# A six-layer decoder on one core: masks of 64 contraction rows in pairs, split first loads, reordered entries into the expert layers, and PSUM banks dealt out anew in the last attention

## The chip, the cores and the metric

The kernel runs on one core of one Trainium2 chip, as one program launched once. The metric is the device time of that launch in microseconds. Before the change it is 1089.61 us, the median of 3 runs (1089.28 to 1089.79).

The engines are named as in the profile: PE is TensorE's matmuls, PEld its weight loads, DVE is VectorE, ACT ScalarE, POOL GpSimd and SP SyncE, which here only issues DMAs.

## What is computed

The input x is 8 batches of 128 tokens with 256 features, the context has the same shape. Six layers follow each other, and after each stands `x = layernorm(x + layer(x))`:

```
A  self-attention, 16 heads of 16, causal
B  attention to the context, 16 heads of 16, plus a residual through relu(x W)
C  experts: 64 of 96 units, the 8 best per token, routed by softmax
D  linear attention in chunks of 64 tokens: running sums of k v and k, gate, rotary embedding
E  attention, 32 query heads of 8 over 8 key heads, keys are the context's and x's,
   scores + ALiBi, window of 64 tokens on the context and 32 on x, then softmax
F  experts: 8 of 176 units, the 2 best per token, plus a shared expert of 704 units with a sigmoid gate
```

The masks of A and E are added to the scores before the softmax: 0 where a key is seen, -1e30 where not. In E only keys up to 64 tokens back are seen. So the 64 early queries of a batch need the early keys only, and the late queries need all of them.

## The kernel before, in words

Every engine has one instruction stream, written out by hand and tied to the others by semaphores. `pe_self_cross` (layers A and B), `pe_moe("C")`, `pe_linear_cross` (D and E) and `pe_moe("F")` are TensorE's; the others have functions of the same kind. Items are batches, and the loops over `t` run stages of different batches side by side.

**Loads.** SyncE issues the constants' and weights' DMAs in groups, `load_weights` (L346): group A (x transposed, head mask, all weights of layer A, and two tiles `v` with their columns of ones), then A2 (causal mask, identities, x by rows), then B, then the first four expert blocks. TensorE, VectorE and ScalarE wait for the whole of group A at their start, TensorE waits for A2 before the first scores, GpSimd for A2 before the first residual.

**Layer A.** One item on TensorE is: keys, values and queries projected (fp32, `pe_T` L411 and `pe_rows` L418), for each of four PSUM banks the causal mask as a bf16 matmul with the identity as weights, 128 rows and 512 columns (L479), then the scores on top, with heads in four row groups of 32 (L485), transposes of the exponentials (L493), values (L524), and output steps (L534, L541). An fp32 matmul has two records in the trace.

**Into an expert layer.** `pe_moe` starts with the routing: the combine weights are transposed in two halves (`pe_combine_T`, L970), ScalarE copies them to `cT`, and `pe_token_weights` (L981) spreads them for the first two blocks. When both halves of `cT` are there, SyncE writes them to DRAM, reads them back spread (L310), and, in layer C, issues all loads of layers D and E (L320) before it refills the expert weights (L284). GpSimd splits every block of weights into a high and a low part (L1977, L1979). A block is 12 matmuls for gate and up (L995) per half of the tokens and 6 for down (L1012). Down accumulates in four banks, which are first cleared by four matmuls with a tile of zeros (L1030).

**Layer D.** `project` begins each of its two halves with a bias matmul of 33 contraction rows in fp32r (L626) and goes on with two fp32 matmuls of 128 rows (L628). `sums` (L647) and `numerators` (L661) use quarters and halves of the array by `tile_position`.

**Layer E.** For each batch there are 12 steps k. In iteration t, scores of one batch (`scores`, for the row maxima, which VectorE reduces, L1649 and L1653) and transposed scores of the batch before it (`scores_T`, of which ScalarE takes the exponentials, L1289) alternate. Steps with k % 3 = 0 are for early queries, the others for late ones. Each begins with a mask matmul of 128 rows and 512 columns (L788 or L796; L829 or L836) and adds the scores with 100 or 102 rows (L792 with four matmuls of 128 columns, L799 with two of 256; L832 and L840 with two of 256). Scores have a ring of two banks, transposed scores of three. Between the steps stand the queries of the next batch (L745, k = 2), its keys and values (L757, L764, k = 4), values (L861, k = 1 and 7), and output steps. SyncE moves each batch's queries and keys between partitions (`spread_queries` L364, 12 DMAs; `spread_keys` L375, 6 DMAs), and then puts the maxima as two rows under the queries (`maxima_rows`, L385); the transposed scores' first step waits for those. VectorE multiplies queries with the head masks (L1637); the scores' first step waits for that.

## Time and profile before

| what | value |
|---|---|
| median of 3 runs | 1089.61 us (1089.28 to 1089.79) |
| the profiled execution | 1087.74 us, its span 1085.9 us |
| mean granted clock of TensorE | 0.96 |
| busy: PE, PEld | 993.8 us (92%), 785.1 us (72%) |
| busy: DVE, ACT, POOL | 617.8 us (57%), 430.2 us (40%), 319.8 us (29%) |
| chain that ended last, by engine | PE 81%, SPq 5%, DVE 5%, issue 3%, DMA 2%, ACT 2%, POOL 1% |
| layers A and B, C, D, E, F, roughly | 0 to 185, 185 to 615, 615 to 710, 710 to 912, 912 to 1086 us |

The profile follows one execution; its times are microseconds from the start of the span. A row of the timeline gives start, duration, engine, line, operation, written and read tiles with their shapes, how many instructions are merged, and, in brackets, how long the engine was idle before and what released it. The chain of waits is followed backwards from the last instruction: each piece is what the end waited for at that time. The ends of matmuls are modelled, their starts are not, so lengths are best read from start to start. At the full granted clock (2.4 GHz) matmuls of 512 columns in fp32r or bf16 follow each other after 0.21 to 0.23 us here (12 of L995 take 2.72 us of the chain), that is about a column per clock, and each of the two records of an fp32 matmul takes about twice that (0.43 us in layer D).

### The profile page before, as it was taken

To read this page: it belongs to the slowest core of one execution; us is meant where nothing else is said; L and a number is where in the kernel's file an instruction comes from. 1 tells how busy PE (TensorE), PEld (TensorE's weight loads), DVE (VectorE), ACT (ScalarE), POOL (GpSimd) and SP (SyncE) were. 2 spreads that over 40 slices of the span, in tenths; PEclk is the share of its full clock that TensorE was granted. 3 is DMA by queue.
4 is the path that set the end of the run, shared out by engine and by line. 5 is a ranking of instruction groups with operands and counts; after the bars stand their busy time and mean duration, and the time that the engine had idled before them with its cause. 6 is when DMAs were issued, how large, how long until landed. Compare 5 with 4: busy or idle time off the path is not lost.

```text
span 1085.9 us, 18386 instructions
## 1 busy us (share of the span) xinstructions
PE 993.8 (92%) x6139; PEld 785.1 (72%) x6148; DVE 617.8 (57%) x1035; ACT 430.2 (40%) x839; POOL 319.8 (29%) x530
## 2 busy tenths in 40 slices
PE   4999997969999999999999689868999998999994
PEld 3778885658888888888888335557787776688883
DVE  2666777435555555555556457554555563455555
ACT  2777785413223223223222223224555554323221
POOL 0033124214443443443444301110000014234431
PEclk9999998989999999999999789978999999899998
DMA  8000000464333333333330000011111101264511
GB/s 298 2 2 2 2 2 2 94 177 140 129 115 117 110 111 119 107 110 120 109 106 15 9 1 1 17 27 27 25 25 31 32 11 59 59 183 106 120 31 39
DMA packets 36950, 75.74 MB, mean 70 GB/s; under 512 B 6844, under 2 KB 17960, under 8 KB 36498
## 3 DMA queue, kind: packets, MB, share of 16 engines
q1 hardware_dynamic: 36606, 74.77, 23.8%
q8 instruction: 34, 0.56, 0.2%
q0 software_dynamic: 288, 0.23, 0.2%
q14 instruction: 22, 0.18, 0.1%
HBM read 67.80 MB, written 2.40 MB: 65 GB/s over the span
## 4 chain that ended last, share of the span: by engine, by line
PE 81%; SPq 5%; DVE 5%; issue 3%; DMA 2%; ACT 2%; POOL 1%; DVEq 0%; POOLq 0%; ACTq 0%
PE ps L995 31%; PE ps L1012 15%; PE ps L411 4%; PE ps L628 3%; PE ps L418 3%; PE ps L493 3%; SPq L364 2%; SPq L320 2%; PE ps L861 2%; PE ps L485 2%; PE ps L524 2%; PE ps L745 1%; PE ps L836 1%; PE ps L840 1%; PE ps L796 1%
## 5 line engine op out<-in xcount | busy, mean ns | idle before, releaser
L995 PE MATMUL ps<-shared 128*128 128x512 f32 x1560 | 381.2, 394 | 9.5 <-POOL shared L1979 9.5
L995 PEld LDWEIGHTS ps<-shared 128*128 128x128 f32 x1560 | 296.9, 191 | 74.0 <-issue 11.7
L1397 ACT ACTIVATE shared<-pT 128x512 fp32r<-128x512 f32 x130 | 82.1, 632 | 287.4 <-DVE pT L1815 287.4
L1977 POOL CAST shared<-wraw 128x512 fp32r<-128x512 f32 (+1 forms) x130 | 92.0, 708 | 315.1 <-PE ps L1012 288.5
L1818 DVE TENSOR_TENSOR al<-pT,shared 128x512 fp32r<-128x512 f32 x130 | 117.1, 901 | 104.3 <-ACT shared L1397 104.3
L1012 PE MATMUL ps<-shared 128*128 128x512 f32 x520 | 162.4, 394 | 1.3 <-DVE al L1818 1.2
L1807 DVE TENSOR_TENSOR e<-e,ps 128x512 f32<-128x512 f32 x130 | 89.3, 687 | 128.4 <-PE ps L995 128.1
L1979 POOL TENSOR_TENSOR shared<-wraw,shared 128x512 fp32r<-128x512 f32 (+1 forms) x130 | 132.3, 1017 | 10.4
L1873 POOL TENSOR_SCALAR newton<-agg 128x1 f32<-128x1 f32 (+1 forms) x36 | 9.1, 254 | 384.1 <-DVE agg L1442 357.5
L1012 PEld LDWEIGHTS ps<-shared 128*128 128x128 f32 x520 | 98.4, 190 | 23.4 <-DVE al L1818 2.1
L1391 ACT ACTIVATE e<-ps 128x512 f32<-128x512 f32 x130 | 77.7, 597 | 84.3 <-PE ps L995 84.2
L1815 DVE TENSOR_TENSOR pT<-e,kbd 128x512 f32<-128x512 f32 x130 | 99.0, 761 | 10.0 <-DMA kbd<-combine_C 3.0
L1012 PE MATMUL ps<-al,shared 128*128 128x512 f32 x260 | 101.8, 392 | 0.0
L1012 PEld LDWEIGHTS ps<-al,shared 128*128 128x128 f32 x260 | 49.2, 189 | 10.3
L1458 DVE TENSOR_REDUCE mx<-ps 128x8 f32<-128x1024 f32 x32 | 39.0, 1220 | 22.2 <-PE ps L485 22.2
L1653 DVE TENSOR_REDUCE mcol<-ps 128x2 f32<-128x512 f32 x64 | 43.2, 677 | 6.0 <-PE ps L799 5.7
L411 PE MATMUL ps<-c_x_t,arena 128*128 128x128 f32 x192 | 28.2, 291 | 14.4 <-DMA v<-in_A_ones_v 12.4
L1137 ACT ACTIVATE pT<-ps 128x512 f32<-128x512 f32 x64 | 36.4, 598 | 8.0 <-PE ps L493 7.9
L799 PE MATMUL ps<-kT,shared 100*128 100x256 f32 x128 | 39.4, 391 | 0.0
L1466 DVE TENSOR_TENSOR e<-ps,mx 128x1024 f32<-128x1024 f32 x32 | 39.0, 1220 | 0.6
L411 PEld LDWEIGHTS ps<-c_x_t,arena 128*128 128x128 f32 x192 | 24.5, 197 | 20.3 <-DMA v<-in_A_ones_v 12.4
L1289 ACT ACTIVATE e<-ps 128x512 f32<-128x512 f32 x48 | 28.4, 595 | 26.6 <-PE ps L832 14.9
(225 smaller groups left out, 1447.5 us busy)
## 6 DMA issues: line engine op xcount, KB each, us to landing
kbd<-combine_C SPq DMA_DIRECT2D x46, 512.0 KB
wraw<-in_C_w SPq DMA_DIRECT2D x48, 384.0 KB, 8.1
kbd<-combine_F SPq DMA_DIRECT2D x15, 512.0 KB
wraw<-in_F_w SPq DMA_DIRECT2D x17, 384.0 KB, 7.1
kbd<-kbd SPq DMA_DIRECT2D x96, 32.0 KB, 1.9
kT<-kbd SPq DMA_DIRECT2D x48, 32.0 KB, 1.8
c_x_t<-in_x_t SPq DMA_DIRECT2D x1, 1024.0 KB, 4.9
c_x_rows<-in_x_rows SPq DMA_DIRECT2D x1, 1024.0 KB, 7.0
```

The lines of the kernel that those rows point to most:

```text
L411: mm = pe.matmul(dst[:, c * P:(c + 1) * P], w[:, k, c * P:(c + 1) * P], src[:, k, :], start=(k == 0), stop=(k == C - 1))
L799: mm = pe.matmul(bank[:, o * D:(o + 1) * D], q_[0:KR, g, 1, o * P:(o + 1) * P], k_[t][0:KR], start=False, stop=True, skip_group_check=True)
L995: mm = pe.matmul(GU[t][s], w[u][:, (c * 2 + s) * P:(c * 2 + s + 1) * P], xx[:, c, t * HALF:(t + 1) * HALF], start=(i == 0), stop=(i == 5))
L1012: mm = pe.matmul(Y[:, 2 * m + t, :], w[u][:, (4 + m) * P:(5 + m) * P], x_[t][:, :], start=False, stop=False, skip_group_check=True)
L1391: act.activation(sgt[t], GU[t][0], ACT.Silu).then_inc(S("silu"), 1)
L1397: act.activation(ah[t][:, :], a2[t], ACT.Copy).then_inc(S("ah"), 1)
L1653: dve.reduce_max(m4[:, g0 + k % 3 - 1, 1, :], SRING[n % 2].rearrange("p (o k) -> p o k", o=2), AX.X)\
L1807: dve.tensor_tensor(a1[t], sgt[t], GU[t][1], ALU.mult).then_inc(S("m_a1"), 1)
L1815: dve.tensor_tensor(a2[t], a1[t], wbc[k][:, t * HALF:(t + 1) * HALF], ALU.mult)\
L1818: dve.tensor_tensor(al[t][:, :], a2[t], ah[t][:, :].bitcast(F32), ALU.subtract)\
L1977: pool.tensor_copy(wh[u][:, lo:hi], wraw[k][:, lo:hi]).then_inc(S("m_wh"), 1)
L1979: pool.tensor_tensor(wl[u][:, lo:hi], wraw[k][:, lo:hi], wh[u][:, lo:hi].bitcast(F32), ALU.subtract).then_inc(S("m_wl"), 1)
```

## The change

It has five parts. (1) The causal mask is now one tile of 128 x 128 per parity of the bank (the second one has its halves of rows swapped); each bank gets it by two matmuls of 64 rows and 64 output partitions, which lie in quarters of the array. (2) In layer E all masks lie in one tile `windows`, by query in partitions 0 to 63, by key in 64 to 127. A score mask uses rows 0 to 63 and a transposed-score mask rows 64 to 127, both 128 output partitions wide, and they are issued one behind the other; steps with k % 3 other than 0 are cut in two halves of 256 columns, each with its own masks and scores. All waits of both kinds stand ahead of the masks. (3) Scores have three banks, transposed scores two. (4) The first loads are four groups A0 to A3, and the ones in `v` are written by GpSimd. Layer B's masked biases are made at t = 6 instead of t = 2. (5) At the entries into the expert layers, gate and up matmuls are cut in two and issued in another order, down begins its banks with `start` instead of the four clearing matmuls, and ScalarE's `high` comes earlier.

```diff
-            load_weights("A")
-            load_weights("A2")
+            for group in ("A0", "A1", "A2", "A3"):
+                load_weights(group)
...
+        XT = sb("c_x_t", [P, C, T])
+        loads["A0"] = [(XT[:, :, 0:2 * P], a["x_t"][:, :, 0:2 * P])]
+        hmask = const("A0", "head_mask")
+        causal = [const("A2", f"causal{h}_bf16", BF16) for h in range(2)]
...
+        loads["A2"].append((X[:, 0:2, :], a["x_rows"][:, 0:2, :]))
+        loads["A3"] = [(XT[:, :, 2 * P:], a["x_t"][:, :, 2 * P:]), (X[:, 2:, :], a["x_rows"][:, 2:, :])]
...
+        for group, names in (("A0", "wk bk"), ("A1", "wv bv wq bq"), ("A2", "bo wo")):
...
-        smask = [const("E", f"smask{h}_bf16", BF16) for h in range(2)]
-        tmask = [const("E", f"tmask{h}_bf16", BF16) for h in range(2)]
+        windows = const("E", "windows_bf16", BF16)
...
-        SRING = [ps[:, 1 + n, :] for n in range(2)]
-        TRING = [ps[:, 3 + n, :] for n in range(3)]
+        SRING = [ps[:, 1 + n, :] for n in range(3)]
+        TRING = [ps[:, 4 + n, :] for n in range(2)]
...
                     for r in range(4):
-                        pe.matmul(ps[:, r, :], ident16[:, :], causal[:, :], start=True, stop=False, skip_group_check=True)
+                        for n in range(2):
+                            rows, out = bass.ds(64 * n, 64), 64 * (n ^ r % 2)
+                            pe.matmul(ps[out:out + 64, r, :], ident16[rows, rows], bc(causal[r % 2][rows, :], 1, 4),
+                                      start=True, stop=False, tile_position=(64 * n, out), skip_group_check=True)
...
+                if t == 2 * B + 3:
+                    pe.wait_ge(S("pc"), 8 * B)
+                    pe_gate_up(pe, "C", 0, 0, 0, (0,))
                 if lo:
                     values(t - 3, 1)
...
-                    pe.wait_ge(S("pc"), 8 * B)
-                    pe_gate_up(pe, "C", 0, 0, 0)
...
+            def scores_mask(b, k, h):
...
+                if k % 3 == 0:
+                    pe.matmul(SRING[n % 3], windows[0:64, 0:P], bc(windows[0:64, P:2 * P], 1, 4),
+                              start=True, stop=False, tile_position=(0, 0), skip_group_check=True)
+                else:
+                    pe.matmul(SRING[n % 3][:, h * D:(h + 1) * D], windows[0:64, 0:P], windows[0:64, 2 * P:4 * P],
+                              start=True, stop=False, tile_position=(0, 0), skip_group_check=True)
...
+            def scores_T_mask(b, k, h):
...
+                    if n >= 2:
+                        pe.wait_ge(S("E_exp"), n - 1)
...
+                lo, n_q, at_ = (0, 8, 0) if k % 3 == 0 else (P + h * P, 4, h * D)
+                pe.matmul(TRING[n % 2][:, at_:at_ + n_q * 64], windows[64:128, lo:lo + P],
+                          bc(ident16[64:128, 64:128], 1, n_q), start=True, stop=False, tile_position=(64, 0),
+                          skip_group_check=True)
...
-                    if es is not None:
-                        scores(es, k)
-                    if ev is not None:
-                        scores_T(ev, k)
+                    for h in range(1 if k % 3 == 0 else 2):
+                        if es is not None:
+                            scores_mask(es, k, h)
+                        if ev is not None:
+                            scores_T_mask(ev, k, h)
+                        if es is not None:
+                            scores(es, k, h)
+                        if ev is not None:
+                            scores_T(ev, k, h)
...
-            gate_up(0, 0, 1)
-            gate_up(1, 1, 0)
+            if L == "C":
+                pe_gate_up(pe, L, 0, 0, 0, (1,))
+            pe_gate_up(pe, L, 0, 0, 1, (0,))
             pe_combine_T(pe, BEFORE[L], 1)
+            pe_gate_up(pe, L, 0, 0, 1, (1,))
             pe_token_weights(pe, L, 0, 1)
             pe_token_weights(pe, L, 1, 1)
-            before_done(pe, L)
-
-            pe.wait_ge(S("zero16"), 1)
-            pe.wait_ge(S("m_spread"), 4 * (L == "F") + 4)
-            for m in range(4):
-                pe.matmul(Y[:, m, :], ident16[:, :], zero16[:, :], start=True, stop=False, skip_group_check=True)
+            gate_up(1, 1, 0)
+            pe.wait_ge(S("m_spread"), 4 * (L == "F") + 2)
             down(0, 0, 0)
             gate_up(1, 1, 1)
+            before_done(pe, L)
+            pe.wait_ge(S("m_spread"), 4 * (L == "F") + 4)
             down(0, 0, 1)
...
             act_combine_T(act, BEFORE[L], 1)
+            high(0, 0)
             act_token_weights(act, L, 0, 1, 3)
+            gate(0, 1)
             act_token_weights(act, L, 1, 1, 4)
+            high(0, 1)
             before_done(act, L)
-            high(0, 0)
-            gate(0, 1)
-            high(0, 1)
...
-            loaded(pool, "A")
+            for u in range(2):
+                pool.memset(v[u][:, :], 0.0).then_inc(S("v_one"), 1)
+            pool.wait_ge(S("v_one"), 2)
+            for u in range(2):
+                pool.memset(v[u][:, :].rearrange("p (h w) -> p h w", w=VW)[:, :, DH0:DH0 + 1], 1.0).then_inc(S("v_one"), 1)
```

The other lines of the diff place the waits: values and queries of item 0 wait for A1 (ScalarE's and VectorE's parts of them too), keys of item 2 and the residual of item 2 for A3.

## Rows read from the trace of the kernel before

**Rows 1.** The chain of waits, first microseconds (start, duration, what).

```profile
6.31 6.07 DMA v<-in_A_ones_v
```

**Rows 2.** Timeline, TensorE and SyncE, entry into layer C.

```profile
200.52 0.60 PE L970 MATMUL ps<-c_ident,oT 128*64 128x128 f32 x4
...
227.44 0.90 SPq L320 DMA_DIRECT2D c_smask_bf<-in_smask_bf  x2
...
238.26 4.55 PE L995 MATMUL ps<-shared 128*128 128x512 f32 x12 [9.49 <-POOL shared L1979]
```

**Rows 3.** Busy time by engine, one steady batch of layer E (stretch, its length, PE busy, ...).

```profile
765.20:788.20 23.00, 21.63 (x196) 17.93 (x195) 13.56 (x27) 12.19 (x25) 2.62 (x6) 1.00 0.13 29
```

**Rows 4.** Timeline, SyncE's queue, steady batch of layer E.

```profile
767.55 8.43 SPq L364 DMA_DIRECT2D kbd<-kbd  x12
...
780.58 0.53 SPq L385 DMA_DIRECT2D shared<-mlo  x1
```

**Rows 5.** DMA issues of the whole run (times issued, KB each, us to landing).

```profile
shared<-mlo SPq DMA_DIRECT2D x16, 8.0 KB, 1.8
...
arena<-in_A_wk SPq DMA_DIRECT2D x1, 256.0 KB, 5.5
```

**Rows 6.** The chain of waits, steady batch of layer E.

```profile
773.51 0.40 PE ps L792 x4
...
774.38 0.23 PE ps L796
774.62 0.23 PE ps L799 x2
774.85 0.23 PE ps L836
775.09 0.24 PE ps L840 x2
...
783.34 0.38 PE ps L788
```

**Rows 7.** Timeline, TensorE's matmuls in layer D.

```profile
664.67 0.67 PE L661 MATMUL ps<-oT,qT 64*64 64x128 f32 x16
...
666.28 1.98 PE L628 MATMUL ps<-arena,c_x_t 128*128 128x512 f32 x4
668.20 0.50 PE L626 MATMUL ps<-shared 33*128 33x512 f32 x1
668.63 1.99 PE L628 MATMUL ps<-arena,c_x_t 128*128 128x512 f32 x4
```

**Rows 8.** Timeline, TensorE's weight loads in the same stretch.

```profile
667.25 0.19 PEld L628 LDWEIGHTS ps<-arena,c_x_t 128*128 128x128 f32 x1 [0.24 <-issue]
668.20 0.18 PEld L626 LDWEIGHTS ps<-shared 33*128 33x128 f32 x1 [0.76 <-issue]
```

**Rows 9.** Who waited for whom, TensorE, 765.2 to 788.2 us (total, times, longest).

```profile
PE ps L788 <- DVE shared L1637: 1.4, 1, 1.4
```

**Rows 10.** The chain of waits, end of layer E's second iteration.

```profile
757.66 1.78 DMA shared<-mlo
```

**Rows 11.** Timeline, TensorE, around the causal masks of one item.

```profile
53.10 1.10 PE L493 MATMUL ps<-c_ident,e 128*128 128x128 f32 x8
...
54.99 1.15 PE L485 MATMUL ps<-kbd,qT 32*128 32x256 f32 x16
```

**Rows 12.** Timeline of the first 30 us: SyncE, GpSimd, TensorE.

```profile
2.27 0.43 SPq L346 DMA_DIRECT2D arena<-in_A_wk  x1
...
15.90 1.40 POOL L1899 TENSOR_TENSOR xb<-c_x_rows,arena 128x256 f32<-128x256 f32 x2 [15.07 <-DMA c_x_rows<-in_x_rows]
...
23.21 1.16 PE L411 MATMUL ps<-c_x_t,arena 128*128 128x128 f32 x8 [0.73 <-ACT kbd L1124]
```

**Rows 13.** Timeline, TensorE, entry into layer F.

```profile
924.17 7.36 PE L995 MATMUL ps<-shared 128*128 128x512 f32 x24
...
943.17 0.62 PE L1012 MATMUL ps<-shared 128*128 128x512 f32 x2
```

152 lines of the change are left out of this document (73 added, 79 removed).

## The prediction

> **What bounds the kernel now.** I read the chain of waits first: it is TensorE almost everywhere, with few exceptions, and the change touches three of them. The first is the start. Nothing is computed until 12.38 us, when the last tile of the first load group lands [rows 1]. The others are the entries into the two expert layers, where TensorE stops, in layer C for 9.49 us [rows 2]. In the last attention (715 to 907 us) a batch of the steady part takes 23.0 us and TensorE is busy for 21.63 of it [rows 3], so there what TensorE does more or less moves the end, unless a second chain is as long. There is one: the queue of SyncE. It begins with a batch's queries, issues 18 copies and then the two rows of maxima, the last at 780.58, which lands some 1.8 us later, near 782.4 [rows 4, 5]; the transposed scores of the next batch start about 0.6 us after the mask at 783.34 [rows 6]. That leaves 1 to 1.5 us of slack per batch.
>
> **Masks, last attention (the large term).** Before, each step has four parts in the chain: mask 0.23, scores 0.23, mask 0.23, transposed scores 0.24, 0.93 in all [rows 6]; a step with k % 3 = 0 has 0.40 for its scores, and so 1.09. A mask costs its 512 columns, 0.21. Now both masks have 64 rows, one in the upper and one in the lower half of the array, and run together; that saves 0.21 per step. But between them and the scores (100 or 102 rows) the array changes from 64-row tiles to the whole and back: twice in a k % 3 = 0 step, four times in the others, which are cut in halves.
>
> What such a change costs is in the linear attention, where a bias matmul of 33 rows stands between fp32 matmuls of 128 rows with no wait between them. The four fp32 ones are 0.43 apart by the weight loads (the last at 667.25), with 0.11 for the first weights: 666.28 + 0.11 + 4 x 0.427 = 668.10. The 33-row weights start at 668.20 [rows 7, 8]: 0.10 later, and not pulled ahead. The bias matmul streams 512 columns (0.21), yet the next 128-row matmul starts at 668.63: 0.43, that is 0.11 of its own weights, 0.21, and 0.10 again; then 0.11 of fp32 weights stand open once more. So going in costs 0.10 plus open weights, and coming out 0.21. I take in 0.14 for bf16 (0.04 of open weights is what a mask has today too) and out 0.21.
>
> A half step is then 0.14 + 0.107 (256 columns, both masks) + 0.02 + 0.21 + 0.107 + 0.107 = 0.69, a step 1.37 against 0.93: +0.43. A k % 3 = 0 step is 0.14 + 0.213 + 0.02 + 0.21 + 0.43 + 0.22 = 1.24 against 1.09: +0.15. Eight and four of them, less 0.3 where a change of tiles stood already (behind values and keys): 3.44 + 0.60 - 0.30 = 3.7 per batch. Of this 0.6 is hidden at k = 9 to 11, where TensorE waits for VectorE's head masks, 1.4 us per batch [rows 9]. That makes 3.1 for each of the six steady batches, 18.6. The batch before them waits for SyncE's copies and maxima rows (landing at 759.44 [rows 10]) and takes part of it: 2.9. In the first, with scores alone, all is hidden but k = 0 to 2: 1.0. In the last, with transposed scores alone, no mask has a partner: a step grows from 0.47 to 2 x (0.14 + 0.107 + 0.21 + 0.107) = 1.13, eight times, and by 0.31 four times, 6.5, of which 1.4 falls into waits for ScalarE: 5.1. Together **+27.6**.
>
> From both sides: if a change cost nothing, each step would save 0.21; if the two masks did not run together either, 0.2 more per step, 2.6 per batch. I take the value of the 33-row matmul, the nearest row by shape.
>
> **Banks.** Two banks for transposed scores instead of three: the mask of step n now waits for the exponential of n - 2. That takes about 0.6 on ScalarE plus 0.25 of handover, and TensorE's step n - 1 takes 1.24 or more, so nothing is added (without the tile cost, steps of 0.72 would lose some 0.15 each in bare stretches). The wait stands ahead of the scores, so VectorE's maxima would be late with it. Three banks for scores remove no wait in the chain.
>
> **Causal masks, layer A.** Before: four of 512 columns, and 1.01 from the end of the transposes (53.10 + 0.88) to the head matmuls at 54.99 [rows 11]. After: eight quarter-array matmuls. The numerators of the linear attention, 16 records of 0.107 on four quarters, take 0.67 with their tail, where two at once would need 0.86 [rows 7]: four run together. So 0.10 + 0.04 + 2 x 0.213 + 0.09 = 0.66, -0.35 on seven items (item 0 waits for its queries): **-2.4**. The quarters of the numerators write a bank per row half; here the two halves write one bank at once, which no row shows. Bound: in turn, five slots of 0.213, +0.29 each, +2.0.
>
> The Trainium skill, TensorEngine Tiling, Restrictions and Gotchas, says that different row tiles cannot access the same PSUM bank at the same time and that software must see to it. By that rule this term is at best the +2.0.
>
> **First loads.** The first group is now an eighth of the work: x of two batches, head mask, keys' weights, four issues 0.47 apart, so the last at about 2.3 (wk's at 2.27 was the fourth before) [rows 12]. It lands between 1.8 us later, as a small copy does, and 5.5, as wk did among 2.8 MB [rows 5]. With 0.5 MB in flight I take 3: 5.3 instead of 12.38, **-7.1** (bounds -8.2 and -4.6). Next in line: the second group at about 7.7, wanted at 7.5; the third (identities, x rows, wo) at about 10.6, wanted by the scores at 11.4; the fourth, 1.5 MB, by bytes at about 14 (now 4.1 MB were in at 15.9), wanted by the third batch's keys at 23.21 - 7.1 = 16.1 [rows 12]. GpSimd's four memsets replace two loads and lie in the wait. No new wait, then. Moving layer B's bias mask to t = 6 keeps VectorE from waiting for layer B's load.
>
> **Into layer C.** What ends last is not TensorE: the combine transpose at 200.52 gives cT, SyncE writes it out, issues the loads of D and E, and only then refills the experts' weights; TensorE waits for their split until 238.26 [rows 2]. So all other savings there (four zero matmuls, 0.9; the first gate part pulled into a wait) count only as far as they bring cT forward. Twelve of the 24 matmuls ahead of the transpose go behind it, 2.6, and the transposes of the last batch no longer queue behind twelve slow ones; a colder clock takes part back. I take -3.0 (bounds -2.0 and -4.7). Four mask loads become one: 0.90 for two issues, so 3 x 0.5 = -1.5. **-4.5**.
>
> **Into layer F** nothing on SyncE is late, so TensorE's own time counts. From 924.17 to 943.17 [rows 13] it takes 19.0 us for 42 wide matmuls (9.2 at 0.22), two spreads (1.9) and a transpose (0.4). The rest is waits, four zero matmuls and slow clock. With only 6 ahead of the transpose, the other work lies in those waits: 2.6 + 0.5 + 1.4 + 2.2 + 2.6 + 1.3 + 2.6 = 13.2, -5.8; I keep 0.8 of it as a wait: **-5.0** (bounds -3 and -6).
>
> **Sum:** -7.1 - 2.4 - 4.5 - 5.0 + 27.6 = +8.6. The profiled execution took 1087.7 (span 1085.9), 1.9 under the median of 1089.6, so 1096.3 there and **1098** against the median. A measurement of this kernel can tell about 0.2% (2.2 us) from no change.
>
> **Rivals.** (a) *Not slower: the change of tiles is free.* Its place is each step of the last attention, its price now 0.35 there and back; it decides from about 0.28 per round trip downwards, where the sum is nought (some 130 round trips on the path, 8.6 / 130 less than 0.35). For it: no bf16 matmul of 64 rows stands in the trace. Against: both ends of the 33-row matmul pay it, and it is fp32r as the scores are [rows 7, 8]. Then the steady batches gain 0.2 in k = 0 to 2 and, behind that, only SyncE's slack: about -1.2 each, with edges -6.6 in all, not -18; causal -3.2. Sum -25, **1064**. The Trainium skill, TensorE: Matmul & The Clock Gate, Part 2, says weight loads are pulled ahead of running matmuls into a background buffer; by that rule it would come out near here, and the trace disagrees at 668.20. (b) *The two halves of a causal mask cannot share a bank*, +4.4: **1102**. (c) *The mask pair does not run together*: 2.6 more in each of seven batches, less what waits hide, **1115**.
>
> **Chances.** Forecast 0.62 (own range 1087 to 1110: the bounds of the start and of the two entries, a round trip of 0.28 or 0.40), (a) 0.22, (b) 0.09, (c) 0.07. Faster: (a) and 0.07 of the forecast, 0.29; same 0.07; slower 0.64. The range takes in (a) and (b): 1060 to 1110.
>
> **What would show it.** TensorE's first matmul at 5 to 5.5; the causal masks' group 0.5 long; cT near 198 less the shift and the wait before the fifth block still 8 us or more; a steady batch of 26.1 (or 21.8 in (a)), with the scores' weight loads starting 0.1 after the masks' streams, not before. A steady batch under 24 would prove me wrong.

## The result and the profile after

The changed kernel takes **1114.86 us** (median of 4 runs, 1112.33 to 1118.68) where the kernel before, on the same chip, takes 1089.44 (1085.05 to 1089.79). The ratio is 1.0246, 95% interval 1.0203 to 1.0288: slower by 25 us by the medians and by 27 by the ratio, where I had forecast 9. The profiled execution of the changed kernel is the slowest of the four, 1118.68 with a span of 1116.9, 31.0 over the span before.

The page of the kernel after: busy times, and the granted clock in 40 slices.

```profile
PE 1050.5 (94%) x6300; PEld 791.3 (71%) x6300; DVE 621.3 (56%) x1034; ACT 432.5 (39%) x839; POOL 319.9 (29%) x534
...
PEclk9999996989999999999998699779899998899998
```

TensorE is busier, and its clock is lower in more places. The lines have moved: L1020 are gate and up, L1006 the spreads, L995 the combine transposes, L1037 down, L801 and L845 the two masks of a half step, L815 and L859 its scores and transposed scores.

**The start.** TensorE's timeline, kernel after (start, duration, engine, line, operands, the idle time ahead and its releaser):

```profile
5.40 2.08 PE L411 MATMUL ps<-c_x_t,arena 128*128 128x128 f32 x8 [5.40 <-DMA arena<-in_A_bk]
8.12 2.07 PE L418 MATMUL ps<-arena,c_x_t 128*128 128x256 f32 x4 [0.64 <-DMA arena<-in_A_bq]
...
17.49 1.16 PE L411 MATMUL ps<-c_x_t,arena 128*128 128x128 f32 x8 [0.72 <-ACT kbd L1151]
...
47.20 0.63 PE L485 MATMUL ps<-c_causal_bf,c_ident_bf 64*64 64x512 bf16 x8
47.75 1.15 PE L492 MATMUL ps<-kbd,qT 32*128 32x256 f32 x16
```

The first matmul is at 5.40, 7.0 earlier than in [rows 1]. But the third projection of keys, at 23.21 in [rows 12], comes only 5.7 earlier. The causal masks of the later items stand 0.55 ahead of the next matmuls (47.20 to 47.75).

**Into layer C.** The same view:

```profile
177.71 2.80 PE L1020 MATMUL ps<-shared 128*128 128x512 f32 x6 [0.70 <-POOL shared L1999]
...
184.51 0.97 PE L995 MATMUL ps<-c_ident,oT 128*64 128x128 f32 x4 [1.61 <-DVE oT L1828]
...
186.16 3.77 PE L1006 MATMUL ps<-cT,c_sel_C 64*128 64x512 f32 x4
...
195.03 0.60 PE L995 MATMUL ps<-c_ident,oT 128*64 128x128 f32 x4
...
231.28 5.12 PE L1020 MATMUL ps<-shared 128*128 128x512 f32 x12 [7.64 <-POOL shared L2014]
```

The fifth block starts at 231.28 against 238.26 in [rows 2], 7.0 earlier. Layers A and B had brought 8.2 (a projection of the last item at 145.66, before at 153.83), so the reordered entry, meant to bring 4.5, lost 1.2. The early gate part (177.71) waits for GpSimd and runs at half pace, with the transposes of x and the routing behind it. Then TensorE waits 1.61 for VectorE's routing (184.51), and from 184.5 to 195 the granted clock is 0.50: the two spreads (L1006, four matmuls) take 3.7 from start to the next start, where they took 1.9 before. The second combine transpose, at 195.03 against 200.52 in [rows 2], has only 5.5 of the 8.2 left.

**Last attention.** Windows of four steady batches, kernel after (stretch, its length, busy time and count of PE, PEld, DVE, ACT and POOL, granted clock, DMA share, GB/s), which answer to [rows 3]:

```profile
763.90:792.70 28.80, 27.97 (x212) 18.39 (x211) 14.21 (x27) 12.47 (x25) 2.61 (x6) 0.87 0.09 23
792.70:821.30 28.60, 27.77 (x212) 18.92 (x211) 13.58 (x27) 12.42 (x26) 2.62 (x6) 0.89 0.09 23
821.30:848.60 27.30, 26.46 (x213) 17.58 (x212) 13.91 (x27) 12.66 (x26) 2.61 (x6) 0.94 0.10 24
848.60:875.80 27.20, 26.37 (x212) 17.47 (x212) 13.79 (x27) 12.55 (x26) 2.61 (x6) 0.94 0.10 24
```

A batch takes 27.2 to 28.8 where I expected 26.1, and its clock is no longer 1.00. TensorE's timeline in one of them shows both parts of the loss:

```profile
812.05 0.28 PE L801 MATMUL ps<-c_windows_bf 64*128 64x256 bf16 x1
812.05 0.28 PE L845 MATMUL ps<-c_ident_bf,c_windows_bf 64*128 64x256 bf16 x1
812.26 0.38 PE L815 MATMUL ps<-kT,shared 100*128 100x256 f32 x1
812.48 0.28 PE L859 MATMUL ps<-shared,kT 102*128 102x256 f32 x1
812.70 0.28 PE L801 MATMUL ps<-c_windows_bf 64*128 64x256 bf16 x1
...
814.24 0.37 PE L798 MATMUL ps<-c_windows_bf 64*128 64x512 bf16 x1 [0.83 <-DVE shared L1667]
...
816.75 0.58 PE L815 MATMUL ps<-kT,shared 100*128 100x256 f32 x1
817.13 0.42 PE L859 MATMUL ps<-shared,kT 102*128 102x256 f32 x1
817.48 0.64 PE L881 MATMUL ps<-pT,vE 128*32 128x256 f32 x2
```

The two masks start together, so the pair does run side by side. A half step is 812.70 - 812.05 = 0.65, of which three streams of 256 columns are 0.32 (0.107 each): the round trip, from 64-row tiles to the whole array and back, costs 0.33 with the weight loads that it leaves open. TensorE's weight loads say where, in another step of the same kernel:

```profile
801.24 0.09 PEld L801 LDWEIGHTS ps<-c_windows_bf 64*128 64x128 bf16 x1
801.24 0.09 PEld L845 LDWEIGHTS ps<-c_ident_bf,c_windows_bf 64*128 64x128 bf16 x1
801.45 0.19 PEld L815 LDWEIGHTS ps<-kT,shared 100*128 100x128 f32 x1
801.56 0.19 PEld L859 LDWEIGHTS ps<-shared,kT 102*128 102x128 f32 x1
801.89 0.09 PEld L801 LDWEIGHTS ps<-c_windows_bf 64*128 64x128 bf16 x1
```

The masks' streams start at 801.24 and need 0.107; the scores' weights load at 801.45, 0.10 behind their end, not during them; those of the transposed scores load while the scores run (801.56). The other part begins behind the wait of 0.83 that ends at 814.24: at 816.75 a score and its transposed one are 0.38 apart instead of 0.22 (812.26 to 812.48), and the values (L881) take 2.41 instead of the 1.43 that they take at the full clock. That is a granted clock of 0.50, 1.2 GHz. In windows of 1 us it stands from about 816 to 820 here, and from 785 to 796 in the first of the four batches.

**Where 31.0 us went**, from the starts of the same work in the two profiled executions:

| stretch | forecast | measured |
|---|---|---|
| layers A and B (start and causal masks) | -9.5 | -8.2 |
| entry into C, to the fifth block | -4.5 | +1.2 |
| rest of C, and layer D | 0 | +1.7 |
| first queries of E to F's first spread (687.62 to 955.13, before 692.94 to 922.26) | +27.6 | +38.2 |
| from that spread to the end | -5.0 | -1.8 |
| sum | +8.6 | +31.0 |

Such rows compare one execution with one. How far a row moves by itself shows in experiment 11, whose code is that of the kernel before up to layer E, but for one load of masks instead of four: the projection that stands at 153.83 before is at 155.35 there, and from it to the fifth block it takes 86.4 instead of 84.4. Differences of 1 to 2 us in a row, the +1.7 among them, are no finding by themselves.

### The profile page after: what moved, and what is told of

Its sections match the earlier page's. It is cut to its first block, busy times and chain, and to the rows that moved or that the text cites. A ratio compares the mean times of both kernels' runs of the same rounds, so it can differ in the third digit from the quotient of the medians.

```text
span 1116.9 us, 18702 instructions
## 1 busy us (share of the span) xinstructions
PE 1050.5 (94%) x6300; PEld 791.3 (71%) x6300; DVE 621.3 (56%) x1034; ACT 432.5 (39%) x839; POOL 319.9 (29%) x534
## 4 chain that ended last, share of the span: by engine, by line
PE 85%; DVE 5%; SPq 4%; issue 2%; DMA 2%; ACT 1%; POOL 1%; POOLq 0%; DVEq 0%; ACTq 0%
PE ps L1020 31%; PE ps L1037 15%; PE ps L411 4%; PE ps L636 3%; PE ps L815 3%; PE ps L881 3%; PE ps L500 3%; PE ps L418 2%; PE ps L801 2%; PE ps L812 2%; SPq L320 2%; PE ps L492 2%; PE ps L859 2%; PE ps L531 2%; PE ps L753 2%
## 5 line engine op out<-in xcount | busy, mean ns | idle before, releaser
L1020 PE MATMUL ps<-shared 128*128 128x512 f32 x1560 | 385.5, 397 | 8.3 <-POOL shared L2014 7.6
L1020 PEld LDWEIGHTS ps<-shared 128*128 128x128 f32 x1560 | 298.6, 192 | 75.9 <-issue 13.5
L1037 PE MATMUL ps<-shared 128*128 128x512 f32 x520 | 160.6, 390 | 1.4 <-DVE al L1848 1.2
L1037 PEld LDWEIGHTS ps<-shared 128*128 128x128 f32 x520 | 97.4, 188 | 22.7 <-DVE al L1848 2.1
L1037 PE MATMUL ps<-al,shared 128*128 128x512 f32 x260 | 101.3, 390 | 0.0
L1037 PEld LDWEIGHTS ps<-al,shared 128*128 128x128 f32 x260 | 48.8, 188 | 10.1
L815 PE MATMUL ps<-kT,shared 100*128 100x256 f32 x128 | 53.3, 416 | 0.0
L845 PE MATMUL ps<-c_ident_bf,c_windows_bf 64*128 64x256 bf16 (+1 forms) x160 | 49.7, 311 | 1.4 <-DMA shared<-mlo 1.4
L1316 ACT ACTIVATE pT<-ps 128x512 f32<-128x512 f32 x48 | 28.7, 597 | 33.8 <-PE ps L859 20.8
L859 PE MATMUL ps<-shared,kT 102*128 102x256 f32 x128 | 39.7, 310 | 0.0
L500 PE MATMUL ps<-c_ident,e 128*128 128x128 f32 x256 | 38.4, 285 | 1.2 <-ACT pT L1164 0.8
```

The costliest lines, as they stand in the source:

```text
L500: mm = pe.transpose(PT[h][:, q * P:(q + 1) * P], e[u][:, at_:at_ + P], ident[:, :])
L815: mm = pe.matmul(bank[:, h * D:(h + 1) * D], q_[0:KR, g0 + k % 3 - 1, 1, h * P:(h + 1) * P], k_[t][0:KR], start=False, stop=True, skip_gro ...
L859: mm = pe.matmul(bank[:, h * D:(h + 1) * D], k_[t][0:KM, (1 - h) * P:(2 - h) * P], q_[0:KM, g0 + k % 3 - 1, 1], start=False, stop=True, sk ...
L1020: mm = pe.matmul(GU[t][s], w[u][:, (c * 2 + s) * P:(c * 2 + s + 1) * P], xx[:, c, t * HALF:(t + 1) * HALF], start=(i == 0), stop=(i == 5))
L1037: mm = pe.matmul(Y[:, 2 * m + t, :], w[u][:, (4 + m) * P:(5 + m) * P], x_[t][:, :], start=(first(x) and i == 0), stop=False, skip_group_ch ...
```

## The experiments

All times are medians, with the ratio to the kernel before on the same chip; before varied from 1080.6 to 1092.6 there.

**1. Last attention as before.** The diff of layer E turned back, the rest of the change kept.

```diff
-        windows = const("E", "windows_bf16", BF16)
+        smask = [const("E", f"smask{h}_bf16", BF16) for h in range(2)]
+        tmask = [const("E", f"tmask{h}_bf16", BF16) for h in range(2)]
...
-        SRING = [ps[:, 1 + n, :] for n in range(3)]
-        TRING = [ps[:, 4 + n, :] for n in range(2)]
+        SRING = [ps[:, 1 + n, :] for n in range(2)]
+        TRING = [ps[:, 3 + n, :] for n in range(3)]
...
```

> The changed kernel with the last attention's masks, their order, their banks and their four loads as before. Theory (the loss is all in the masks of the last attention): the linear attention starts 6.4 us earlier than before, as in the changed kernel, a steady batch is 23.0 again at a granted clock of 1.00, and the whole is 1078 to 1084 us. Rival (part of the loss sits in the entry to layer F or in the reordered transitions): steady batches of 23.0, but the whole stays at 1088 or more.

Measured: 1076.83 us, ratio 0.9901 (0.9867 to 0.9936). Its windows:

```profile
783.90:806.90 23.00, 21.63 (x197) 17.93 (x196) 13.40 (x27) 12.35 (x26) 2.62 (x6) 1.00 0.13 29
```

The batch of [rows 3] is back. The whole loss lies in the last attention, and without it the change wins 10 us. From F's first spread to the end it takes 158.5 against 163.6 before, 5.1 less. That is the best case: in the other profiled executions with the new entry the same stretch takes 160.0 to 161.7, and in those with the old one 163.6 to 165.6.

**2. Halved steps, masks of 128 rows.**

```diff
-                    pe.matmul(SRING[n % 3][:, h * D:(h + 1) * D], windows[0:64, 0:P], windows[0:64, 2 * P:4 * P],
-                              start=True, stop=False, tile_position=(0, 0), skip_group_check=True)
+                    pe.matmul(SRING[n % 3][:, h * D:(h + 1) * D], ident16[:, :], smask[1][:, :], start=True, stop=False,
+                              skip_group_check=True)
```

(and so for the other three masks)

> The changed kernel with its halved steps, its order and its banks (three and two), but with masks of 128 contraction rows instead of 64, so nothing in a step changes the tiles of the array. Theory (the change of tiles is the cost): four masks of 0.107 us in a step instead of two pairs, a step 0.93 to 1.0, a steady batch 23 to 24, the whole 1078 to 1088 us. Rival (halving the steps, or two banks for the transposed scores, is the cost): a steady batch stays at 27 or more, the whole at 1105 or more.

Measured: 1081.95 us, ratio 0.9952 (0.9923 to 0.9981).

```profile
786.30:809.70 23.40, 21.88 (x213) 18.08 (x212) 13.74 (x27) 12.37 (x26) 2.62 (x6) 1.00 0.13 28
```

Halves, order and banks together cost 0.4 per batch. The other 3.8 to 5.4 of the changed kernel hang on the 64 rows. Here a batch leaves TensorE idle for 1.5, and the clock stays at 1.00.

**3. Whole steps with masks of 64 rows.**

```diff
-                    for h in range(1 if k % 3 == 0 else 2):
+                    halves = range(1 if k % 3 == 0 else 2)
+                    for h in halves:
                         if es is not None:
                             scores_mask(es, k, h)
                         if ev is not None:
                             scores_T_mask(ev, k, h)
-                        if es is not None:
+                    if es is not None:
+                        for h in halves:
                             scores(es, k, h)
-                        if ev is not None:
+                    if ev is not None:
+                        for h in halves:
                             scores_T(ev, k, h)
```

> The changed kernel with both halves' masks ahead of both halves' scores: one change of tiles there and back in a step instead of two. Theory (about 0.31 us per round trip): a step with k % 3 != 0 falls from 1.30 to about 1.0 us, eight of them a batch, so 2.5 us less in each of seven batches, 17 us in all, and 1095 to 1100 us, less if the clock stays up as well. Rival (the price hangs on the 64-row matmuls themselves, not on the changes): the same 1115 us.

Measured: 1105.06 us, ratio 1.0178 (1.0129 to 1.0228); the profiled execution had a span of 1096.3. In this kernel the mask of a step's first half is left out of the sum (see 7); the matmuls are the same. A whole step in TensorE's timeline:

```profile
825.36 0.28 PE L801 MATMUL ps<-c_windows_bf 64*128 64x256 bf16 x1
825.37 0.28 PE L845 MATMUL ps<-c_ident_bf,c_windows_bf 64*128 64x256 bf16 x1
825.48 0.27 PE L801 MATMUL ps<-c_windows_bf 64*128 64x256 bf16 x1
825.48 0.27 PE L845 MATMUL ps<-c_ident_bf,c_windows_bf 64*128 64x256 bf16 x1
825.68 0.50 PE L815 MATMUL ps<-kT,shared 100*128 100x256 f32 x2
826.02 0.40 PE L859 MATMUL ps<-shared,kT 102*128 102x256 f32 x2
```

From the first masks to the scores it is 0.32 and from there to the transposed scores 0.34. With 0.22 for their streams and 0.10 to the next masks a step is 0.98 to 0.99 (experiment 7 has two back to back, 794.05 to 795.04), where two halves are 1.30: 0.31 less for one round trip less. The price hangs on the change of tiles. The total moved by 10 us by the medians, less than the 17 expected, for two reasons. At the full clock a batch takes 23.91, which is 1.8 less than the 25.7 of experiment 4 and not 2.5, since the wait for the head masks grows to 1.44. And two of the four steady batches (26.94 and 25.38) still had a lower clock, behind this wait:

```profile
785.15 0.37 PE L798 MATMUL ps<-c_windows_bf 64*128 64x512 bf16 x1 [1.44 <-DVE shared L1670]
```

Of its five such waits two were followed by a low clock and three were not.

**4. Filling matmuls, 128 rows.** Four of them, 0.21 each, where TensorE waits for VectorE's head masks.

```diff
+                    if k == 0 and b >= 2:
+                        for _ in range(4):
+                            pe.matmul(SRING[n % 3], ident16[:, :], bc(ident16[:, :], 1, 4), start=True, stop=False,
+                                      skip_group_check=True)
```

> The changed kernel with four more matmuls of 128 rows and 512 columns (0.85 us together) in each batch from the third on, in the place where TensorE waits 0.83 us for VectorE's head masks; the mask writes over what they leave. Theory (the granted clock falls behind that wait): the stretch of 3 to 10 us at 1.2 GHz after it goes, a steady batch falls from 27.2 to 28.8 to about 26.7, five or six of them, so 6 to 10 us less, 1105 to 1109 us. Rival (the clock falls for what the batch does as a whole, or the excess is a wait): the slow stretches stay, 1114 to 1119 us.

Measured: 1104.96 us, ratio 1.0151 (1.0093 to 1.0209). The windows:

```profile
763.00:788.70 25.70, 25.70 (x216) 17.28 (x215) 13.93 (x27) 12.31 (x24) 2.61 (x6) 1.00 0.10 25
788.70:814.40 25.70, 25.70 (x216) 17.27 (x215) 13.82 (x27) 12.59 (x25) 2.61 (x6) 1.00 0.10 26
814.40:840.20 25.80, 25.80 (x216) 17.27 (x215) 13.83 (x27) 12.59 (x25) 2.62 (x6) 1.00 0.10 26
```

More work, and 1.5 to 3.1 us less per batch: all slow stretches of the steady part are gone. From the first queries to F's first spread it takes 256.0, against 229.3 before, **+26.7**; the other 11.5 of the 38.2 were the clock behind the waits. The 26.7 are not all at the full clock: from the first queries to the last ones the periods are -0.2, +2.4, +0.9 and four times +2.7 against before, and from the last queries on it is +12.8. In the first two periods and at the end some 41 us still run at 1.2 GHz, where before it was 24.

**5. Filling matmuls, 64 rows.**

```diff
-                            pe.matmul(SRING[n % 3], ident16[:, :], bc(ident16[:, :], 1, 4), start=True, stop=False,
-                                      skip_group_check=True)
+                            pe.matmul(SRING[n % 3], windows[0:64, 0:P], bc(windows[0:64, P:2 * P], 1, 4),
+                                      start=True, stop=False, tile_position=(0, 0), skip_group_check=True)
```

> The changed kernel with four filling matmuls in front of VectorE's head masks, of 64 rows and 512 columns instead of 128 rows. Theory (it is the idle time that brings the clock down): as with 128 rows, steady batches of 25.7 and 1105 us. Rival (matmuls on half the rows of the array do not hold the clock up): the slow stretches stay in at least half of the batches, steady batches of 26.5 to 28.8, 1110 us or more.

Measured: 1104.28 us, ratio 1.0141 (1.011 to 1.0172), steady batches again 25.7:

```profile
787.00:812.70 25.70, 25.70 (x217) 17.26 (x216) 13.83 (x27) 12.58 (x26) 2.61 (x6) 1.00 0.10 26
```

Matmuls on half the rows hold the clock as well. Without the idle time it does not fall here, whatever the rows of the filler.

**6. The early gate part put back.** On top of experiment 1.

```diff
-                if t == 2 * B + 3:
-                    pe.wait_ge(S("pc"), 8 * B)
-                    pe_gate_up(pe, "C", 0, 0, 0, (0,))
...
                     pe_logits(pe, "B", (5,))
+                    pe.wait_ge(S("pc"), 8 * B)
+                    pe_gate_up(pe, "C", 0, 0, 0, (0,))
```

> The changed kernel with the last attention's masks as before, and the early gate part of layer C put back behind the logits of the sixth batch (still half a gate there). Theory (the early gate part waits for GpSimd, runs 6 matmuls in 2.6 us at 1.2 GHz and delays the transposes of the last two batches of x): the combine transpose of the second half comes 1.5 to 3 us earlier than at 195.98, the fifth block with it, 1073 to 1075 us against 1076.8. Rival (what is late there is VectorE's routing, whatever TensorE does ahead of it): the same within 1 us.

Measured: **1069.55 us**, ratio 0.9816 (0.9777 to 0.9856), against 0.9901 in experiment 1; more than either theory gave. TensorE's timeline:

```profile
183.59 0.88 PE L978 MATMUL ps<-c_ident,oT 128*64 128x128 f32 x4
...
185.15 1.98 PE L989 MATMUL ps<-cT,c_sel_C 64*128 64x512 f32 x4 [0.29 <-ACT cT L1387]
187.06 3.03 PE L1003 MATMUL ps<-shared 128*128 128x512 f32 x12
189.93 0.60 PE L978 MATMUL ps<-c_ident,oT 128*64 128x128 f32 x4
...
226.13 2.07 PE L1003 MATMUL ps<-shared 128*128 128x512 f32 x4 [7.62 <-POOL shared L1997]
```

The second combine transpose is at 189.93, against 195.98 in experiment 1, and the fifth block at 226.13 against 232.84. Of these 6.7 us 1.7 are no work of the edit, as they are there more than 30 us ahead of it: the last item's projection is at 145.00 here and at 146.66 in experiment 1. From it to the first combine transpose it is 38.6 here and 38.9 there, so the early part held up the routing by 0.3 at most. The rest, 4 to 5 us, is clock: there the spreads take 3.78 and the 12 matmuls behind them 5.49, here 1.98 and 3.03.

In its old place the gate part (179.71 to 182.42) fills the time in which VectorE routes; moved ahead, it leaves a wait of 1.61 there. The two orders differ in every profiled execution: with the early part the first two spreads take 3.71 from their start to the next matmul (seven kernels), without it 1.91 (seven, the kernel before among them). That the wait is what lowers the clock there is not tested by a filler.

The total moved by 7.3 us by the medians; in the profiled execution layers C and D also had less of the low clock by chance (10 us of it between 600 and 635, against 27 in experiment 1).

**7. Whole steps, one start flag, and the filler.** Of two masks that open a bank of transposed scores only the first has the start flag.

```diff
-                          bc(ident16[64:128, 64:128], 1, n_q), start=True, stop=False, tile_position=(64, 0),
+                          bc(ident16[64:128, 64:128], 1, n_q), start=(h == 0), stop=False, tile_position=(64, 0),
```

(the scores' mask is one matmul of 512 columns, and the filler is that of experiment 4)

> The changed kernel with both halves' masks ahead of both halves' scores, one mask of 512 columns for the scores, and of the two masks of the transposed scores only the first with the start flag (with the flag on both, what the first one wrote did not count: it was left out of the sum in the kernel with whole steps); and with the four filling matmuls ahead of VectorE's head masks. Theory (round trips and clock are the two parts of the loss, and add): steady batches of 23.9 to 24.1 from the third on at a granted clock of 1.00, 1090 to 1096 us. Rival (the two gains overlap): 1100 or more.

Measured: 1088.98 us, ratio 0.9997 (0.9977 to 1.0017): the whole change with masks in pairs is as fast as the kernel before.

```profile
778.60:802.50 23.90, 23.34 (x208) 16.16 (x207) 13.69 (x27) 12.36 (x25) 2.62 (x6) 1.00 0.11 28
```

Round trips and clock add up, and all masks count in the sum. The filler fills 0.85 of the wait and leaves 0.56 of it, and the batch is as long as those of experiment 3 at a clock of 1.00 (23.91). In experiment 3, where the second mask of a bank had the flag too, the first one's did not. The Trainium skill, PSUM — Partial Sum Buffer, The four PSUM rules, says that a matmul with the start flag clears the written bits of the whole bank in the 32-partition quadrants it writes; the two kernels agree with that. It also bears out the changed kernel's order: with a flag on each half, the scores of the first must be in before the mask of the second.

**8. First loads and causal masks alone.** Before, with both entries and the last attention untouched.

```diff
-            load_weights("A")
-            load_weights("A2")
+            for group in ("A0", "A1", "A2", "A3"):
+                load_weights(group)
...
-                        pe.matmul(ps[:, r, :], ident16[:, :], causal[:, :], start=True, stop=False, skip_group_check=True)
+                        for n in range(2):
+                            rows, out = bass.ds(64 * n, 64), 64 * (n ^ r % 2)
+                            pe.matmul(ps[out:out + 64, r, :], ident16[rows, rows], bc(causal[r % 2][rows, :], 1, 4),
+                                      start=True, stop=False, tile_position=(64 * n, out), skip_group_check=True)
```

> Before, with only the split first loads and the causal masks in quarters; both entries and the last attention as before. Theory: 8.2 us less from layers A and B; the reordered entry to layer C was worth little (lost 1.2 to 3 us by the trace) and that to layer F 5 us, so this one is 1079 to 1082 us where before is 1087 and the one with both entries reordered 1076.8. Rival (the entry to C did bring its gain, hidden by a colder clock): 1083 or more.

Measured: 1080.21 us, ratio 0.9918 (0.9887 to 0.9949). Its interval overlaps that of experiment 1, so both entries reordered, with the gate part early, are worth nothing that can be told; by experiment 6, with the gate part late, they are worth about 1%. (The profiled execution here is the slowest of its six, 1087.51, with 24 us at 1.2 GHz at the end of layer B.)

**9. First loads alone.**

```diff
-                        for n in range(2):
-                            rows, out = bass.ds(64 * n, 64), 64 * (n ^ r % 2)
-                            pe.matmul(ps[out:out + 64, r, :], ident16[rows, rows], bc(causal[r % 2][rows, :], 1, 4),
-                                      start=True, stop=False, tile_position=(64 * n, out), skip_group_check=True)
+                        pe.matmul(ps[:, r, :], ident16[:, :], bc(causal[0][:, :], 1, 4), start=True, stop=False,
+                                  skip_group_check=True)
```

> Before, with only the split first loads; the causal masks are four matmuls of 128 rows again. Theory: TensorE starts at 5.4; from the masks of one item to the matmuls behind them 0.95 us or more instead of 0.55, so that with the masks in quarters an item of layer A is 0.3 to 0.4 us shorter, and the first item of layer B comes 5.5 us earlier than before, not 7.85. Rival (the quarters bring nothing that the end sees): 7.5 or more earlier here as well.

One run: 1088.49 us, where before takes 1086.73 (1081.89 to 1087.22) on that chip: no verdict on the total. TensorE's timeline:

```profile
11.04 2.07 PE L413 MATMUL ps<-c_x_t,arena 128*128 128x128 f32 x8 [0.78 <-ACT kbd L1133]
12.90 1.91 PE L485 MATMUL ps<-c_causal_bf,c_ident_bf 128*128 128x512 bf16 x4
14.74 1.78 PE L492 MATMUL ps<-kbd,qT 32*128 32x256 f32 x16
...
19.21 1.16 PE L413 MATMUL ps<-c_x_t,arena 128*128 128x128 f32 x8 [0.73 <-ACT kbd L1133]
...
49.80 1.03 PE L485 MATMUL ps<-c_causal_bf,c_ident_bf 128*128 128x512 bf16 x4
50.76 1.15 PE L492 MATMUL ps<-kbd,qT 32*128 32x256 f32 x16
```

From the masks to the matmuls behind them it is 0.96, in quarters 0.55. From the second item's masks to the seventh's it is 47.72 us here and 46.22 in the changed kernel, 0.30 per item; from the first item's to the second's, at a slower pace, 8.84 here and 7.87 in experiment 8. Of the 6.4 us by which the first matmul (6.03) comes earlier, 4.0 are left at the third projection of keys (19.21 against 23.21): the second projection (11.04, 2.07 for 8) and the first masks (12.90, 1.91 for 4) still run at half pace, where before the second one took 1.16 and the first masks 1.03. The first item of layer B comes 4.2 earlier (77.92 against 82.14), not 5.5.

How long the half pace lasts changes from execution to execution, though. In experiment 11, whose start is that of the kernel before, the first masks are slow too:

```profile
19.18 1.78 PE L478 MATMUL ps<-c_causal_bf,c_ident_bf 128*128 128x512 bf16 x4
24.73 1.16 PE L410 MATMUL ps<-c_x_t,arena 128*128 128x128 f32 x8 [0.73 <-ACT kbd L1140]
```

There the third projection is at 24.73, 12.4 behind the first matmul, and before 10.8. In the twelve kernels with the new loads it is 10.7 to 13.2. So a loss of up to 2 us behind the earlier start is possible, and none is shown.

**10. The whole change with both faults of the clock mended** (filler of experiment 4, gate part of experiment 6).

```diff
-                if t == 2 * B + 3:
-                    pe.wait_ge(S("pc"), 8 * B)
-                    pe_gate_up(pe, "C", 0, 0, 0, (0,))
...
+                    if k == 0 and b >= 2:
+                        for _ in range(4):
+                            pe.matmul(SRING[n % 3], ident16[:, :], bc(ident16[:, :], 1, 4), start=True, stop=False,
+                                      skip_group_check=True)
...
+                    pe.wait_ge(S("pc"), 8 * B)
+                    pe_gate_up(pe, "C", 0, 0, 0, (0,))
```

> The whole change with its two clock faults mended: four filling matmuls ahead of VectorE's head masks, and the early gate part of layer C behind the logits again. Theory (my sum was right for a clock at 2.4 GHz; its misses are the clock in the steady batches and the early gate part): 1105 less 7, so 1096 to 1100 us, about the forecast of 1098. Rival (the 7 us of the gate part were not its own): 1103 to 1106.

Measured: 1099.49 us, ratio 1.0112 (1.0076 to 1.0148). The interval overlaps that of experiment 4, 1.0093 to 1.0209, so the gain of the late gate part on top of the filler is not shown by the totals; its spreads take 1.91 again, as in experiment 6. Before takes 1086.73 on this chip, so the time is 12.8 over it. By the rows of the profiled execution, against before: layers A and B -7.4, the entry into C -5.0, the rest of C and D +3.4, the last attention +26.3, the rest -3.5.

**11. The last attention's masks alone.** Before, with only the edits that experiment 1 takes back, the other way round.

```diff
-                    if es is not None:
-                        scores(es, k)
-                    if ev is not None:
-                        scores_T(ev, k)
+                    for h in range(1 if k % 3 == 0 else 2):
+                        if es is not None:
+                            scores_mask(es, k, h)
+                        if ev is not None:
+                            scores_T_mask(ev, k, h)
+                        if es is not None:
+                            scores(es, k, h)
+                        if ev is not None:
+                            scores_T(ev, k, h)
...
```

> Before, with only the last attention's masks, order and banks as changed. Theory (all of the loss is here, 27 us of changes of tiles and 8 to 13 of clock): 1089 + 36 to 39, so 1123 to 1129 us. Rival (the loss hangs on the entries as well, the order of the first gate part above all): 1112 or less.

Measured: 1128.38 us, ratio 1.0375 (1.0342 to 1.0407): 42 us over before on the same chip (1086.73). That agrees with the changed kernel over experiment 1 (1.0246 / 0.9901 = 1.0348). From the first queries to F's first spread it takes 266.8, as the changed kernel's 267.5; that is 37.5 of the 42.9 us by which the profiled execution is longer, and the other 5.4 lie in stretches that the edit leaves alone but for the load of the masks. One steady batch:

```profile
802.90:831.40 28.50, 27.67 (x212) 18.27 (x211) 13.77 (x27) 12.54 (x25) 2.61 (x6) 0.88 0.09 23
```

**12. Fillers at two waits for copied keys**, on top of experiment 6.

```diff
+                if k == 0 and b < 2:
+                    for _ in range((24, 14)[b]):
+                        pe.matmul(bank, ident16[:, :], bc(ident16[:, :], 1, 4), start=True, stop=False,
+                                  skip_group_check=True)
```

> The fastest version so far (first loads, causal masks in quarters, entries reordered but the early gate part late, last attention as before) with 24 and 14 filling matmuls of 0.21 us in the two places of 6.97 and 4.00 us where TensorE waits for the copied keys. Theory (the clock is at 1.2 GHz for 10 and 13 us behind these waits, where TensorE is busy most of the time): 2 to 5 us less, 1065 to 1068. Rival (SyncE's copies set the pace in these two batches, not TensorE): the same 1069.5, or slower where a filler stands in the way.

Measured: 1067.75 us, ratio 0.9833 (0.981 to 0.9857); experiment 6 has 0.9816 with an interval around it. The first three periods of the last attention took 68.5 us instead of 73.2 in the two profiled executions, but the totals can't be told apart, as this execution had more of the low clock at the end of layer C and in layer D (about 27 us of it against 10), which the filler doesn't touch. Open.

## Why the prediction was wrong

The direction and the main mechanism were right; 1098 was 17 us short of 1114.86, and the range ended at 1110. The measured time is the 1115 of rival (c), but by chance: its condition is false (see below).

**The change of tiles** was right, and its size nearly so. I took 0.35 for a round trip from the 33-row matmul [rows 7, 8]; the trace gives 0.33 and the difference of whole and half steps 0.31. My half step of 0.69 is 0.65. With the steady batches at the full clock the last attention costs +26.7 (experiment 4) where the sum had +27.6. Here some luck is in the total: a steady batch costs +2.7 instead of +3.1, and the beginning and the end of the attention, with more of the low clock, cost the more. The Trainium skill, TensorEngine Tiling (Array Packing), Key Properties, says that changing the tiling mode drains TensorE; it gives no price, and the trace agrees, with 0.31 to 0.33 there and back. Rival (a), a free change, is out (its own terms add up to -26.4, not to -25). So is rival (c): the pair starts at one time (812.05 twice).

**The step that failed most: the clock behind a wait that hides part of the cost.** I wrote that 0.6 per batch "is hidden at k = 9 to 11, where TensorE waits for VectorE's head masks". The hiding was right: the wait shrinks from 1.37 to 0.83. What failed is that I costed all batches at 2.4 GHz and put the clock behind that wait at nothing, since before the batches had a granted clock of 1.00 with 1.4 us of the same wait. In the changed kernel the clock falls behind what is left of it, 0.83, all five times: 3.4 to 10 us at 1.2 GHz each. That is 1.5 to 3.1 us per batch and 11.5 us in all, shown by the filler (experiments 4 and 5). With the 26.7 it makes the 38.2. Why the same engine with a longer wait (1.37 and 1.52, five times each) kept its clock before, and in experiment 2, is open: what differs is the 64-row masks and the bare weight loads round them. With half the changes of tiles and a wait of 1.44 (experiment 3) it fell two times of five. The filler shows only that without the wait it does not fall.

**The entry into layer C** failed in one phrase: "the first gate part pulled into a wait" was counted as a saving (or nothing), and "a colder clock takes part back" as small. The part went ahead of the transposes of x, with a wait of 0.70 for GpSimd of its own, and left TensorE idle where VectorE routes. The routing is hardly later for it (0.3), but the clock is low through the first two spreads and the gate part behind them, 4.1 us: +1.2 instead of -4.5. With the part back in its place the fifth block starts at 226.13 (experiment 6), 12.1 before the 238.26 of [rows 2]; less the 8.8 by which layers A and B are ahead in that execution (145.00 against 153.83) that is -3.3, and -5.0 and -5.2 in experiments 10 and 12. So the -4.5 was right for that order; the wait ahead of that block is 7.6 to 8.5 there.

**The entry into layer F:** -5.0 was forecast, -5.1 measured in experiment 1, -3.5 in most other executions and -1.8 in the changed kernel. In the last the spreads take 2.90 and the gate parts 2.93 and 4.62, at 1.2 GHz again; to name what lowers the clock there, in the last steps of the attention, I have no experiment.

**First loads:** -7.1 as a start (measured -7.0), but only 4.0 to 5.7 of it is left at the third projection in the executions shown. I had let everything behind the start move with it. TensorE begins at half pace either way; in the execution before, those slow first microseconds were over by the second projection, and in these they reach through the first masks or scores. Since they last longer in experiment 11 too, with the old loads, it stays open how much of this the earlier start costs. "No new wait" was nearly right: 0.64 at 8.12 for the second group.

**Causal masks:** -0.35 per item forecast, -0.30 measured on five items and about -1.0 on the slow first one (experiments 8 and 9), -2.5 together where I had -2.4. Rival (b) is out: the four quarters that fill two banks start within 0.01 us of each other (at 47.20), so two row tiles write the two halves of one bank at one time. The trace disagrees here with the rule that the prediction cites from the Trainium skill, TensorEngine Tiling (Array Packing), Restrictions and Gotchas. The Trainium skill, PSUM — Partial Sum Buffer, PSUM bank collisions raise a hardware error, repeats that rule, and reports the error as measured where two row tiles write the same bank and the same quadrant of 32 partitions. These halves are in different quadrants, and the 0.55 agrees with that narrower reading.

**Banks:** two banks for the transposed scores, with halves and order, cost 0.4 per batch (experiment 2), not nothing.

With both clock faults mended the kernel takes 1099.49 (experiment 10), near the forecast of 1098. That looks better than it is, as before is faster on that chip too: it is 12.8 over before where I had 8.6, a ratio of 1.0112 (from 1.0076) for one of 1.0077. The fastest kernel here by its ratio is experiment 6, 1069.55 us, 1.8% under the kernel before: first loads, causal masks in quarters and reordered transitions, without the early gate part and with the last attention left as it was.

## What to carry to other kernels

Masks with half the contraction rows pay only where nothing of the whole array stands between them: price each change of tiles at about 0.3 us there and back, and group all that shares a tiling. Where a change makes a dense stretch less dense, ask what the clock does behind its waits before calling a wait a cover; a few idle matmuls in the wait are a cheap test, and here they took back 10 us. A step moved out of one wait into another is not free: look at the clock behind the wait that it leaves empty.

## What the runs showed of the hardware

- A wait of 0.83 us on TensorE was followed by 3.4 to 10 us at 1.2 GHz five times of five in the changed kernel and in experiment 11, and one of 1.44 two times of five in experiment 3, while 1.4 and 1.5 us at the same place were not in two kernels with 128-row masks. Filled with matmuls of 128 or of 64 rows, the clock stayed at 1.00.
- Weight loads were not pulled ahead across a change of tiles: 801.45, 0.10 behind the masks' streams, for fp32r weights, where the next ones load during the matmul before them (801.56). There and back it is 0.31 to 0.33 us.
- Two matmuls with the start flag into two halves of the columns of one bank: the second makes the first one's result be written over by what should add to it (experiments 3 and 7). In different halves of the partitions both may have it (the causal masks).
- TensorE's first microseconds run at half pace (8 fp32 matmuls 2.08 us, later 1.16) though the granted clock is recorded as 1.00 there. With a start at 5.4 to 6.3 us the half pace was over by 11 to 16, with one at 12.3 and 12.4 by 21 (experiment 11) and 17 (before).
- Low-clock stretches move from execution to execution in the same code: at the end of layer B the kernel before had 7 us of it between 175 and 195, experiment 11 had 20 (174 to 195).
